# Differential attention beside an fp8 feed-forward block on one core: square root table loaded by a dummy root, copies of the first stage in another order, last exponentials, scaling and projection by smaller parts

## The chip, the core and the metric

The kernel runs on one core of a Trainium2 chip. The metric is the time of one execution on the device, in microseconds (us). The core has five engines that run side by side, each through its own instructions in order: PE (TensorE, matmuls and transposes), ACT (ScalarE, activation functions and copies), DVE (VectorE, elementwise work and 32x32 transposes), POOL (GpSimd) and SP (here only a queue that issues DMAs). They wait for one another through semaphores: an instruction adds to one when it ends, and a wait holds its engine until the count is reached.

## The reference, cut to what matters

```python
xn   = layernorm(x)                                  # x: 1024 rows x 256
qkv  = xn @ Wqkv                                     # q1,k1,q2,k2 (128 wide each), v (256); 16 heads of 8
A1   = causal_softmax(q1 k1^T / sqrt(8)) v
A2   = causal_softmax(q2 k2^T / sqrt(8)) v
diff = A1 - lam * A2
diff = (1 - LAMBDA_INIT) * diff / sqrt(mean(diff^2, -1) + 1e-5)
attn = diff @ Wproj
ffn  = fp8dot(gelu(fp8dot(xn, Wg0)) * fp8dot(xn, Wg1), Wlin)   # hidden 1024
out  = x + attn + ffn
```

## The kernel before

All engines run programs written out by hand; no scheduler decides an order. There are four stages.

**1. Normalising, transposing, projecting.** x comes in eight blocks of 128 rows, in four DMAs of two blocks (the first pair as two DMAs). For pair i, DVE takes the statistics (`stats_of` L578, `spread_of` L583). ACT takes the square root (`root`, L417), DVE the reciprocal (`even_block`, L589), then DVE normalises the even block (L592) and ACT the odd one (`odd_block`, L424). PE transposes the pair into bank i of PSUM (`transposes`, L882), and ACT copies it from there into `xn_t` (`turned`, L430, semaphore `xt_out`). PE then multiplies with the weights of q1 and k1 (`queries_keys`, L902): units 0 and 1 are done with pairs 0 and 1, units 2 and 3 with pairs 2 and 3. Before its first transpose PE runs 11 matmuls on an identity (`WARM_UP`, L887), and behind it 3 more (`KEEP_UP`, L925). Each unit's sum is split in two: ACT copies its upper bits from PSUM to `parts` (`upper`, L436, `hi_ready`), DVE subtracts these and keeps the rest (`rest`, L616, `low_ready`). DVE also makes xn_t's fp8 copy in two halves (`x_to_fp8`, L621). ACT needs another function table for the gelu of stage 2, and has it loaded by a dummy activation (L455) between `upper(1)` and `upper(2)`.

**2. Feed-forward, upper half.** 16 steps n: four fp8 matmuls on PE (L958) into a pair of banks, gelu on ACT (L472), a product on DVE (L634). Step 0 waits for two `low_ready`, step 1 for four `xt_out`, step 2 for four `low_ready`, since they write the banks that stage 1 still reads. Bounds for the softmax are worked out beside it.

**3. Attention.** 96 units: PE makes three banks of scores (L1038), ACT takes one exponential over 128x1536 (L493), POOL masks the diagonal blocks, and PE multiplies with the values (L1050) some units later. DVE turns and divides the sums (`take` L709, `divide` L715 and L716), subtracts the branches, and POOL and PE do the rest of the projections and the feed-forward's lower half beside it.

**4. Ending.** The last exponential releases the last product (group 7, chunk 8; its four matmuls are 512 wide). DVE then does `take(7, 1)`, the last difference, the mean square; ACT the last root (L510); DVE the reciprocal, `scale_by_root(3, last)` (L753) and `turn_back(1, 1)` (L757). PE's `ending` waits for `turn_back(1, 0)` (third `out_t_ready`), does ten matmuls of the output projection (L1081) and one of the residual (L1086), waits for `turn_back(1, 1)` (fourth) and does the last four (blocks 4 to 7). DVE and ACT add or copy, and DMAs carry the result out.

Of the kernel before, what the change touches and what calls it, by code (L numbers as in the profile page):

```python
# [7 lines left out]
ACT = mybir.ActivationFunctionType  # L8
# [7 lines left out]
P = 128  # L16
T = 1024
C = 256
# [7 lines left out]
BR = 2  # L26
# [41 lines left out]

V_BANK = (6, 7, 6, 7)

WARM_UP, KEEP_UP = 11, 3

Y_BANK = (7, 7, 0, 0, 2, 2, 3, 4)

# [53 lines left out]
def diff_attention_ffn_kernel(nc, x, w_qkv, w_proj, lq1, lk1, lq2, lk2, w_gating, w_linear, out):  # L128
# [3 lines left out]
    with ExitStack() as ctx:  # L132
# [276 lines left out]
        @block.scalar  # L409
        def _(act):  # L410
            act.dma_start(x_sb[:, 1, :], x_rows[:, 1, :]).then_inc(x_in[0], 16)
            for b in (2, 6):
                act.dma_start(x_sb[:, b:b + 2, :], x_rows[:, b:b + 2, :]).then_inc(x_in[b // 2], 16)

            def root(i):
                act.wait_ge(var_ready, 2 * i + 2)
                act.activation(rstd[:, 1, 2 * i:2 * i + 2], mean_var[:, 2 * i:2 * i + 2, 1], ACT.Sqrt, bias=eps[:, 0:1]  # L417
                               ).then_inc(root_ready, 1)

            def odd_block(i):  # L420

                b = 2 * i + 1
                act.wait_ge(moved_ready, i + 1)
                act.activation(xn[:, b, :], x_sb[:, b, :], ACT.Identity, bias=rstd[:, 3, b:b + 1],  # L424
                               scale=rstd[:, 2, b:b + 1]).then_inc(odd_ready, 1)

            def turned(i):

                act.wait_ge(xt_ready, i + 1)
                act.activation(xn_t[:, :, i * C:(i + 1) * C], ps[:, i, :].rearrange("p (k n) -> p k n", k=KC), ACT.Copy  # L430
                               ).then_inc(xt_out, 1)

            def upper(u):
                i, h = QK_UNITS[u]
                act.wait_ge(qk_ready, u + 1)
                act.activation(parts[:, i, 0, h * HALF:(h + 1) * HALF], ps[:, QK_BANK[u], :], ACT.Copy  # L436
                               ).then_inc(hi_ready, 1)

            act.wait_ge(eps_set, 1)
            root(0)  # L440
            odd_block(0)
            turned(0)
            root(1)
            odd_block(1)
            root(2)
            turned(1)
            odd_block(2)
            root(3)
            turned(2)
            odd_block(3)  # L450
            upper(0)
            turned(3)
            upper(1)

            act.activation(lam_w[:, 6:7], rstd[:, 1, 0:1], ACT.Gelu_apprx_tanh)  # L455
            upper(2)
            upper(3)

            def move_longest(u):

                act.activation(norm_most[0:32, 0, u:u + 1], norm_most[32 * u:32 * u + 32, 0, 0:1], ACT.Copy
                               ).then_inc(norms_moved, 1)

            def move_shift(u):

                act.activation(shift[32 * u:32 * u + 32, 0, 1, :], shift[0:32, 0, 1, :], ACT.Copy).then_inc(shift_ready, 1)

            for n in range(len(FFN)):
                act.wait_ge(up_ready, n + 1)
                if n >= RING:  # L470
                    act.wait_ge(hidden_ready, n - RING + 1)
                act.activation(gated[:, n % RING, :], ps[:, 2 * PAIR[n], :], ACT.Gelu_apprx_tanh  # L472
                               ).then_inc(gelu_ready, 1)

                if n == 4:
                    act.wait_ge(norms_taken, 1)
                if 4 <= n < 7:
                    move_longest(n - 3)
                if n == 12:
                    act.wait_ge(shift_low, 1)  # L480
                if 12 <= n < 15:
                    move_shift(n - 11)
            act.wait_ge(dots_ready, 2)
            act.activation(lam_w[:, 2:4], lam_w[:, 0:2], ACT.Exp).then_inc(lam_exp, 1)

            for n in range(UNITS):
                br, hg, at = n // BRANCH, n // STEPS % HG, n * PER_UNIT % (KEPT * J)
                if n % BRANCH == 0:
                    act.wait_ge(shift_ready, 3 * (br + 1))
                if n * PER_UNIT < KEPT * J and at + PER_UNIT > KEPT * J - 2:  # L490
                    act.wait_ge(hidden_ready, len(FFN))
                act.wait_ge(scores_ready, n + 1)
                act.activation(probs[:, at:at + PER_UNIT, :].rearrange("p s u -> p (s u)"),  # L493
                               ps[:, 3 * (n % 2):3 * (n % 2) + 3, :].rearrange("p b n -> p (b n)"),
                               ACT.Exp, bias=shift[:, br, 1, hg * BR + br:hg * BR + br + 1], scale=SCALE
                               ).then_inc(exp_done, 1)

            def whole(b):

                act.wait_ge(y_ready, 4 if b == 6 else 1)  # L500
                at = C if b == 1 else 0
                act.activation(y[:, b, :], ps[:, Y_BANK[b], at:at + C], ACT.Copy).then_inc(y_copied, 1)


            act.activation(newton[:, 1, 112:113], newton[:, 0, 0:1], ACT.Sqrt)
            for b in (0, 1):
                whole(b)
            act.wait_ge(eps_set, 2)
            act.wait_ge(ms_ready, 1)
            act.activation(newton[:, 3, 112:128], newton[:, 2, 112:128], ACT.Sqrt, bias=root_eps[:, 0:1], scale=ROOT_SCALE  # L510
                           ).then_inc(rms_ready, 1)
            whole(6)
            act.wait_ge(y_copied, 3)
            act.dma_start(out_rows[:, 6, :], y[:, 6, :]).then_inc(y_out, 16)
# [58 lines left out]
        def _(dve):  # L573
# [35 lines left out]
            spread_of(3)  # L609
            even_block(3)  # L610

            def rest(u, bank):
                i, h = QK_UNITS[u]
                cols = slice(h * HALF, (h + 1) * HALF)
                dve.wait_ge(hi_ready, u + 1)
                dve.tensor_tensor(parts[:, i, 1, cols], ps[:, bank, :], parts_f32[:, i, 0, cols], ALU.subtract  # L616
                                  ).then_inc(low_ready, 1)

            def x_to_fp8(h):
                dve.wait_ge(xt_out, 2 * (h + 1))  # L620
                dve.tensor_copy(x8[:, :, h * HALF:(h + 1) * HALF], xn_t[:, :, h * HALF:(h + 1) * HALF],  # L621
                                saturate=False).then_inc(x8_ready, 1)

            x_to_fp8(0)
            rest(0, QK_BANK[0])
            x_to_fp8(1)
            rest(1, QK_BANK[1])
            rest(2, QK_BANK[2])
            rest(3, QK_BANK[3])

# [119 lines left out]
            def scale_by_root(i, b):  # L750
                n = b.stop - b.start
                s = slice(32 * i + b.start, 32 * i + b.stop)
                own.step(dve.tensor_tensor(fin[:, b, i, :], attn1[:, i, b, :],  # L753
                                           root[:, s].unsqueeze(2).broadcast_to([P, n, DV]), ALU.mult))

            def turn_back(p, h):
                dve.transpose(out_t[:, p, h * HALF:(h + 1) * HALF],  # L757
                              fin[:, 16 * h:16 * h + 16, 2 * p:2 * p + 2, :].rearrange("p b g d -> p b (g d)")
                              ).then_inc(out_t_ready, 1)

            def values_in(b):
# [79 lines left out]
            inverse_root(slice(0, 64))  # L841
            scale_by_root(0, all_of)
            scale_by_root(1, all_of)
            turn_back(0, 0)
            turn_back(0, 1)
            own.step(difference(2, 0))
            mean_of(2, 0)
            take(6, 1)
# [5 lines left out]
            inverse_root(slice(64, 112))  # L854
            scale_by_root(3, first)
            scale_by_root(2, all_of)
            turn_back(1, 0)
            take(7, 1)
            difference(3, 1).then_inc(ms_ready, 1)
            dve.wait_ge(rms_ready, 1)  # L860
            own.step(dve.reciprocal(root[:, 112:128], u[:, 112:128]))
            scale_by_root(3, last)
            turn_back(1, 1)
            dve.wait_ge(res_ready, TB // 2)
            for b in (2, 4):
                dve.wait_ge(y_ready, b // 2 + 1)
# [6 lines left out]
        def _(pe):  # L873
# [181 lines left out]
            def values(g, c):  # L1055
                if c in DIAGONALS:
                    pe.wait_ge(masked, diagonals_until(g, c))
                else:
                    pe.wait_ge(exp_done, g * STEPS + last_unit(c) + 1)
                (kb, wide, q0), *more = CHUNKS[c]  # L1060

                if g == 0 and c == 0:
                    pe.wait_ge(v_out, 6)
                if c == 0 and g > 0:
                    pe.wait_ge(o_taken, 2 * g)
                ins = product(g, c, 0, kb, wide, q0, c == 0)
                if c in (MIXED, LAST):
                    ins.then_inc(o_ready, 1)
                elif more:
                    product(g, c, wide * P, *more[0], False)  # L1070
# [53 lines left out]
            def ending():  # L1124
# [15 lines left out]
                residual(6)  # L1140
                pe.wait_ge(out_t_ready, 4)
                project(4, 1)
                for b in (5, 6, 7):
                    project(b, 1).then_inc(y_ready, 1)

            def second_branch(general):
# [45 lines left out]
```

## Time and profile before

| | us |
|---|---|
| median of 3 runs | 185.56 (185.2 to 185.72) |
| the profiled execution, its own time | 185.81 |
| its span, first to last instruction | 184.1 |
| ACT busy | 163.2 (89%) |
| PE busy | 177.2 (96%) |
| DVE busy | 90.9 (49%) |
| POOL busy | 63.5 (35%) |

The span is the time between the first and the last instruction of the profiled execution; the 1.7 us beside it lie outside of all instructions. A busy share is an average over the four stages, and PE's records overlap, so it says little of which engine sets the end. For that the chain of waits is read, which follows the last instruction back to what released it. In a timeline a row gives start, length, engine, line, and in brackets the idle time before it with what ended it. An fp32 matmul leaves two records, a matmul in fp8 or bf16 one.

### The profile page before, as it was taken

What the parts mean: (1) busy time and instruction counts of PE and PEld (TensorE: products, weight loads), DVE (VectorE), ACT (ScalarE), POOL (GpSimd) and SP (SyncE); (2) the same over time, 40 slices, a digit from 0 to 9 for tenths busy, and PEclk for the clock granted to TensorE, in tenths of its full rate; (3) what the DMA queues carried; (4) which work ended last, traced back from release to release, by engine and by line L of the source; (5) the groups of instructions that cost most, each with busy time, mean ns of one, the idle gap of its engine ahead of it and who ended that gap; (6) DMA issues with size and microseconds to landing.
All of it is one profiled execution on the core that took longest, in us unless ns stands there. A gap on an engine that the chain in (4) does not pass through costs nothing.

```text
span 184.1 us, 4290 instructions
## 1 busy us (share of the span) xinstructions
PE 177.2 (96%) x1810; PEld 77.3 (42%) x1810; DVE 90.9 (49%) x216; ACT 163.2 (89%) x145; POOL 63.5 (35%) x81
## 2 busy tenths in 40 slices
PE   6899999999999999999999999999999999989992
PEld 6787344443332423243334424334524434433381
DVE  2485879432313150440365022616551789979872
ACT  0678587999999999999999999999999999999810
POOL 8319950051207321450523053307403560323000
PEclk9999999999999999999999999999999999999999
DMA  5987658874000000000087876000000000000015
GB/s 170 382 307 226 164 144 193 213 166 108 0 0 5 0 0 4 0 0 4 15 204 171 207 164 166 0 0 4 4 0 0 4 0 4 0 0 4 0 57 178
DMA packets 8935, 15.02 MB, mean 82 GB/s; under 512 B 2000, under 2 KB 5584, under 8 KB 8912
## 3 DMA queue, kind: packets, MB, share of 16 engines
q1 hardware_dynamic: 8080, 13.92, 27.8%
q10 hardware_dynamic: 832, 0.79, 1.3%
q8 instruction: 16, 0.26, 0.6%
q14 instruction: 7, 0.06, 0.1%
HBM read 5.26 MB, written 1.05 MB: 34 GB/s over the span
## 4 chain that ended last, share of the span: by engine, by line
ACT 77%; PE 18%; DVE 2%; DMA 1%; issue 1%; ACTq 0%
ACT probs L493 74%; PE ps L958 7%; PE ps L1081 4%; PE ps L902 3%; PE ps L892 2%; DMA x_sb<-L_attn_x 1%; PE ps L882 1%; DVE parts L616 1%; ACT L455 1%; ACT L417 1%; PE ps L1050 1%; ACT parts L436 1%; PE ps L1038 0%; DVE stats L578 0%; PE ps L925 0%
## 5 line engine op out<-in xcount | busy, mean ns | idle before, releaser
L493 ACT ACTIVATE probs<-ps,shift 128x1536 f32<-128x1536 f32 x96 | 138.0, 1599 | 0.2 <-PE ps L1038 0.2
L1050 PE MATMUL ps<-probs,v_all 128*32 128x512 f32 (+3 forms) x768 | 78.3, 496 | 1.1 <-DVE o_t L709 0.8
L393 POOL TENSOR_SCALAR_AFFINE_SELECT probs<-probs 128x1024 f32<-128x1024 f32 (+1 forms) x40 | 36.7, 918 | 94.8 <-ACT probs L493 94.8
L1038 PE MATMUL ps<-q_st,k_st 32*128 32x512 f32 (+3 forms) x384 | 48.4, 411 | 0.0
L1038 PEld LDWEIGHTS ps<-q_st,k_st 32*128 32x128 f32 x384 | 22.5, 182 | 61.5 <-ACT probs L493 43.4
L709 DVE STREAM_TRANSPOSE o_t<-ps 128x512 f32<-128x512 f32 x16 | 11.5, 717 | 45.3 <-PE ps L1050 45.2
L1050 PEld LDWEIGHTS ps<-probs,v_all 128*32 128x32 f32 x768 | 16.2, 108 | 18.8 <-issue 9.5
L958 PE MATMUL ps<-area 128*128 128x512 fp8e4 x64 | 14.4, 379 | 0.2 <-DVE parts L616 0.2
L472 ACT ACTIVATE probs<-ps 128x512 bf16<-128x512 f32 x16 | 9.6, 597 | 3.5 <-PE ps L958 2.9
L634 DVE TENSOR_TENSOR area<-ps,probs 128x512 fp8e4<-128x512 f32 x16 | 10.9, 685 | 1.9 <-ACT probs L472 1.8
L355 POOL TENSOR_TENSOR squares<-parts 128x512 bf16<-128x512 f32 x8 | 8.7, 1099 | 2.1 <-DVE parts L773 2.1
L958 PEld LDWEIGHTS ps<-area 128*128 128x128 fp8e4 x64 | 6.0, 97 | 8.1 <-issue 0.9
L892 PE MATMUL ps<-area 128*32 128x256 fp8e4 x256 | 9.2, 273 | 0.0
L892 PE MATMUL ps<-xn_t,w_q 128*32 128x256 f32 (+1 forms) x88 | 9.0, 482 | 0.0
L773 DVE CAST parts<-ps 128x512 fp32r<-128x512 f32 x4 | 2.8, 692 | 12.5 <-PE ps L892 12.5
L892 PE MATMUL ps<-w_q,xn_t 128*32 128x256 f32 x128 | 8.4, 384 | 0.0
L902 PE MATMUL ps<-xn_t,w_q 128*128 128x256 f32 x32 | 7.9, 390 | 0.1
L1081 PE MATMUL ps<-w_p,squares 128*128 128x256 f32 x32 | 7.7, 389 | 0.0
L892 PEld LDWEIGHTS ps<-area 128*32 128x32 fp8e4 x256 | 6.7, 97 | 2.3 <-issue 0.5
L778 DVE CAST ffn<-ps 128x512 bf16<-128x512 f32 x4 | 2.8, 691 | 9.2 <-PE ps L892 9.2
L362 POOL CAST area<-probs 128x512 fp8e4<-128x512 f32 x8 | 4.9, 658 | 6.1 <-DVE probs L592 6.1
L1081 PEld LDWEIGHTS ps<-w_p,squares 128*128 128x128 f32 x32 | 5.8, 190 | 2.0 <-DVE squares L757 1.2
(88 smaller groups left out, 128.0 us busy)
## 6 DMA issues: line engine op xcount, KB each, us to landing
q_st<-parts SPq DMA_DIRECT2D x32, 128.0 KB, 2.7
k_st<-parts SPq DMA_DIRECT2D x32, 128.0 KB, 2.8
probs<-L_ffn_w_gating SPq DMA_DIRECT2D x4, 512.0 KB, 7.3
probs<-L_ffn_w_linear SPq DMA_DIRECT2D x1, 1024.0 KB, 12.7
out<-probs SPq DMA_DIRECT2D x3, 256.0 KB, 2.3
x_sb<-L_attn_x ACTq DMA_DIRECT2D x2, 256.0 KB, 5.0
w_q<-L_attn_Wqkv SPq DMA_DIRECT2D x1, 512.0 KB, 9.1
w_q<-L_attn_Wqkv SPq DMA_DIRECT2D x1, 256.0 KB, 3.8
```

What stands on the lines that cost most here:

```text
L355: pool.tensor_tensor(squares[:, i, cols], parts_f32[:, i, 0, cols], parts_f32[:, i, 0, cols], ALU.mult).then_inc(squared, 1)
L393: pool.affine_select(out=blocks, in_=blocks, pattern=pattern, compare_op=ALU.is_ge, fill=0.0, base=0, channel_multiplier=-1).then_inc(mask ...
L472: act.activation(gated[:, n % RING, :], ps[:, 2 * PAIR[n], :], ACT.Gelu_apprx_tanh).then_inc(gelu_ready, 1)
L493: act.activation(probs[:, at:at + PER_UNIT, :].rearrange("p s u -> p (s u)"), ps[:, 3 * (n % 2):3 * (n % 2) + 3, :].rearrange("p b n -> p ...
L634: dve.tensor_tensor(hidden[:, c, h * HALF:(h + 1) * HALF], ps[:, 2 * PAIR[n] + 1, :], gated[:, n % RING, :], ALU.mult, saturate=False).the ...
L709: dve.transpose(o_t[:, h, :, :].rearrange("p b w -> p (b w)"), ps[:, 6, :]).then_inc(o_taken, 1)
L892: ins = pe.matmul(ps[q:q + 32, bank, at:at + right.shape[-1]], left[:, q:q + 32], right, start=start, stop=stop, skip_group_check=True)
L902: return pe.matmul(ps[:, bank, at:at + wide], w_q[:, k, i * P:(i + 1) * P], xn_t[:, k, h * HALF + at:h * HALF + at + wide], start=(k == 0 ...
L958: ins = pe.matmul(ps[:, 2 * PAIR[n] + g, :], w_gate8[:, g, k, c * P:(c + 1) * P], x8[:, k, h * HALF:(h + 1) * HALF], start=(k == 0), stop= ...
L1038: ins = pe.matmul(ps[:, bank, at:at + wide * P], k_st[rows, g % STACKS, kb * P:(kb + 1) * P], q_st[rows, g % STACKS, queries], start=True, ...
L1050: ins = pe.matmul(ps[32 * j:32 * j + 32, 6, q0 % HALF:q0 % HALF + wide * P], v_all[:, g % HG, kb, 32 * j:32 * j + 32], probs[:, slot + j, ...
L1081: return pe.matmul(ps[:, Y_BANK[b], at:at + C], out_t[:, p, b * P:(b + 1) * P], w_p[:, p, :], start=start, stop=(p == 1), skip_group_check ...
```

## The change

- ACT runs a dummy square root as soon as `eps` is set, before it waits for any statistics.
- `WARM_UP` is 10 instead of 11.
- `turned(3)` is done by DVE, between `rest(0)` and `rest(1)`; `rest(1)` now stands before `x_to_fp8(1)`.
- The dummy gelu stands between `upper(0)` and `upper(1)`.
- The last exponential (n = 95) is two activations of 128x3x256; the last product is two of half the width, each waiting for its own.
- `scale_by_root(3, last)` and `turn_back(1, 1)` are done in two halves of 8 blocks, and PE's last four projections wait in two pairs.

```diff
-WARM_UP, KEEP_UP = 11, 3
+WARM_UP, KEEP_UP = 10, 3
@@ ACT
             act.wait_ge(eps_set, 1)
+            act.activation(lam_w[:, 7:8], eps[:, 0:1], ACT.Sqrt)
             root(0)
...
             upper(0)
-            turned(3)
+
+            act.activation(lam_w[:, 6:7], rstd[:, 1, 0:1], ACT.Gelu_apprx_tanh)
             upper(1)
-
-            act.activation(lam_w[:, 6:7], rstd[:, 1, 0:1], ACT.Gelu_apprx_tanh)
             upper(2)
...
+                for e in range(1 if n < UNITS - 1 else 2):
+                    cols = slice(e * C, (e + 1) * C) if n == UNITS - 1 else slice(0, HALF)
+                    act.activation(probs[:, at:at + PER_UNIT, cols], ps[:, 3 * (n % 2):3 * (n % 2) + 3, cols],
+                                   ACT.Exp, bias=shift[:, br, 1, hg * BR + br:hg * BR + br + 1], scale=SCALE
+                                   ).then_inc(exp_done, 1)
@@ DVE
+            def turned(i):
+
+                dve.wait_ge(xt_ready, i + 1)
+                dve.tensor_copy(xn_t[:, :, i * C:(i + 1) * C], ps[:, i, :].rearrange("p (k n) -> p k n", k=KC)
+                                ).then_inc(xt_out, 1)
...
             rest(0, QK_BANK[0])
+            turned(3)
+            rest(1, QK_BANK[1])
             x_to_fp8(1)
-            rest(1, QK_BANK[1])
             rest(2, QK_BANK[2])
...
-            scale_by_root(3, last)
-            turn_back(1, 1)
+            for b in (16, 24):
+                scale_by_root(3, slice(b, b + 8))
+                turn_back(1, b, 8)
@@ PE
+                if (g, c) == (GROUPS - 1, NC - 1):
+                    product(g, c, 0, kb, 2, q0, False)
+                    pe.wait_ge(exp_done, UNITS + 1)
+                    product(g, c, 2 * P, kb, 2, q0 + 2 * P, False).then_inc(o_ready, 1)
+                    return
...
                 project(4, 1)
-                for b in (5, 6, 7):
+                project(5, 1).then_inc(y_ready, 1)
+                pe.wait_ge(out_t_ready, 5)
+                for b in (6, 7):
                     project(b, 1).then_inc(y_ready, 1)
```

ACT's order at the start and at the end of stage 1. First the program before, from its first DMA; `rstd` is the root's output, `parts<-ps` is `upper`, `xn_t<-ps` is `turned`:

```order
L411 DMA x_sb<-L_attn_x 128x256
L413 DMA x_sb<-L_attn_x 128x2x256 x2
L417 ACT_TABLE_LOAD [waits var_ready]
L417 ACTIVATE rstd<-mean_var,eps 128x2 [waits eps_set]
...
L436 ACTIVATE parts<-ps 128x512 [waits qk_ready]
L430 ACTIVATE xn_t<-ps 128x2x256 [waits xt_ready]
L436 ACTIVATE parts<-ps 128x512 [waits qk_ready]
L455 ACT_TABLE_LOAD
L455 ACTIVATE lam_w<-rstd 128x1
L436 ACTIVATE parts<-ps 128x512 [waits qk_ready] x2
```

And the same places now:

```order
L411 DMA x_sb<-L_attn_x 128x256
L413 DMA x_sb<-L_attn_x 128x2x256 x2
L441 ACT_TABLE_LOAD
L441 ACTIVATE lam_w<-eps 128x1 [waits eps_set]
L417 ACTIVATE rstd<-mean_var,eps 128x2 [waits var_ready]
...
L436 ACTIVATE parts<-ps 128x512 [waits qk_ready]
L455 ACT_TABLE_LOAD
L455 ACTIVATE lam_w<-rstd 128x1
L436 ACTIVATE parts<-ps 128x512 [waits qk_ready] x3
```

The first table load no longer stands behind the wait for the variances, and one copy (`turned(3)`) has left the stretch between the last odd block and the gelus, where the load has moved one place up.

DVE at the end of stage 1, before (from `x_to_fp8(0)` to the first product of the feed-forward):

```order
L621 CAST area<-xn_t 128x2x512 [waits xt_out]
L616 TENSOR_TENSOR parts<-ps,parts 128x512 [waits hi_ready]
L621 CAST area<-xn_t 128x2x512 [waits xt_out]
L616 TENSOR_TENSOR parts<-ps,parts 128x512 [waits hi_ready] x3
L634 TENSOR_TENSOR area<-ps,probs 128x512 [waits gelu_ready] x3
```

and now:

```order
L630 CAST area<-xn_t 128x2x512 [waits xt_out]
L625 TENSOR_TENSOR parts<-ps,parts 128x512 [waits hi_ready]
L618 COPY xn_t<-ps 128x2x256 [waits xt_ready]
L625 TENSOR_TENSOR parts<-ps,parts 128x512 [waits hi_ready]
L630 CAST area<-xn_t 128x2x512 [waits xt_out]
L625 TENSOR_TENSOR parts<-ps,parts 128x512 [waits hi_ready] x2
L644 TENSOR_TENSOR area<-ps,probs 128x512 [waits gelu_ready] x3
```

DVE has one instruction more there, and its second `rest` no longer stands behind the second cast.

PE's last instructions, before (values, projection, residual, projection):

```order
L1050 MATMUL ps<-probs,v_all 32x512 [waits exp_done]
L1050 MATMUL ps<-probs,v_all 32x512 x3
L1081 MATMUL ps<-w_p,squares 128x256 [waits out_t_ready]
L1081 MATMUL ps<-w_p,squares 128x256 x9
L1086 MATMUL ps<-x_sb,ident 128x256 [waits res_ready]
L1081 MATMUL ps<-w_p,squares 128x256 [waits out_t_ready]
L1081 MATMUL ps<-w_p,squares 128x256 x3
```

and now:

```order
L1062 MATMUL ps<-probs,v_all 32x256 [waits exp_done]
L1062 MATMUL ps<-probs,v_all 32x256 x3
L1062 MATMUL ps<-probs,v_all 32x256 [waits exp_done]
L1062 MATMUL ps<-probs,v_all 32x256 x3
L1098 MATMUL ps<-w_p,squares 128x256 [waits out_t_ready]
L1098 MATMUL ps<-w_p,squares 128x256 x9
L1103 MATMUL ps<-x_sb,ident 128x256 [waits res_ready]
L1098 MATMUL ps<-w_p,squares 128x256 [waits out_t_ready]
L1098 MATMUL ps<-w_p,squares 128x256
L1098 MATMUL ps<-w_p,squares 128x256 [waits out_t_ready]
L1098 MATMUL ps<-w_p,squares 128x256
```

The last product has become two of half the width, and the last two projections have a wait of their own; the eleven matmuls between keep their places.

## Rows read from the trace of the kernel before

**Rows 1.** The page: span, and the chain that ended last, by engine.

```profile
span 184.1 us, 4290 instructions
ACT 77%; PE 18%; DVE 2%; DMA 1%; issue 1%; ACTq 0%
```

**Rows 2.** The chain of waits in order of time: start us, us, what.

```profile
4.69 1.28 ACT L417
...
18.02 1.30 DVE parts L616 x2
...
103.55 68.95 ACT probs L493 x48
...
172.54 1.06 PE ps L1050 x8
173.61 4.51 PE ps L1081 x20
178.12 0.43 PE ps L1086 x2
```

**Rows 3.** Timeline of ACT, 0 to 26 us: start us, us, engine, line, what.

```profile
1.24 1.00 ACTq L413 DMA_DIRECT2D x_sb<-L_attn_x  x2
4.69 1.28 ACT L417 ACT_TABLE_LOAD   x1 [4.69 <-DVE mean_var L583]
5.98 0.30 ACT L417 ACTIVATE rstd<-mean_var,eps 128x2 f32<-128x2 f32 x1
...
13.63 0.58 ACT L436 ACTIVATE parts<-ps 128x512 fp32r<-128x512 f32 x1
14.90 0.60 ACT L430 ACTIVATE xn_t<-ps 128x512 f32<-128x512 f32 x1 [0.69 <-PE ps L882]
...
16.00 1.28 ACT L455 ACT_TABLE_LOAD   x1
...
17.41 1.07 ACT L436 ACTIVATE parts<-ps 128x512 fp32r<-128x512 f32 x2
```

**Rows 4.** Timeline of PE, 0 to 30 us.

```profile
1.61 5.06 PE L887 MATMUL ps<-ident 128*128 128x128 f32 x22 [1.61 <-POOL ident L336]
7.05 0.97 PE L882 MATMUL ps<-ident,probs 128*128 128x128 f32 x4 [0.38 <-DVE probs L592]
...
8.80 1.10 PE L902 MATMUL ps<-xn_t,w_q 128*128 128x256 f32 x4
...
17.38 1.89 PE L958 MATMUL ps<-area 128*128 128x512 fp8e4 x8
19.45 1.89 PE L958 MATMUL ps<-area 128*128 128x512 fp8e4 x8 [0.18 <-DVE parts L616]
```

**Rows 5.** PE's lines L887 and L925: ns min/median/max of a record, first and last start.

```profile
L887 PE MATMUL ps<-ident x22: 421/421/582, 1.6 to 6.3; 128*128 128x128 f32 x22
...
L925 PE MATMUL ps<-ident x6: 275/275/275, 7.9 to 8.4; 128*128 128x128 f32 x6
```

**Rows 6.** Tile x_sb: all DMAs into it, issue to landing.

```profile
DMA to landing us min/median/max: 2.3/4.2/5.7
```

**Rows 7.** Timeline of DVE, 0 to 33 us.

```profile
6.59 0.41 DVE L592 TENSOR_SCALAR probs<-x_sb,mean_var,rstd 128x256 f32<-128x256 f32 x1
6.91 0.74 DVE L578 BATCH_NORM_STATS2 stats<-x_sb 128x6 f32<-128x256 f32 x2
...
14.25 0.69 DVE L616 TENSOR_TENSOR parts<-ps,parts 128x512 fp32r<-128x512 f32 x1 [0.77 <-ACT parts L436]
```

**Rows 8.** Timeline of PE's weight loads, 15.0 to 15.7 us.

```profile
15.55 0.30 PEld L902 LDWEIGHTS ps<-xn_t,w_q 128*128 128x128 f32 x2 [0.22 <-ACT xn_t L430]
```

**Rows 9.** Timeline of DVE, 170 to 182 us.

```profile
172.71 0.71 DVE L757 STREAM_TRANSPOSE squares<-xn_t 128x512 f32<-128x512 f32 x1
173.67 0.72 DVE L709 STREAM_TRANSPOSE o_t<-ps 128x512 f32<-128x512 f32 x1 [0.25 <-PE ps L1050]
...
177.29 0.42 DVE L753 TENSOR_TENSOR xn_t<-attn,newton 128x256 f32<-128x256 f32 x1
177.75 0.71 DVE L757 STREAM_TRANSPOSE squares<-xn_t 128x512 f32<-128x512 f32 x1
```

**Rows 10.** The page's groups: out<-in xcount, busy us, mean ns of one.

```profile
L493 ACT ACTIVATE probs<-ps,shift 128x1536 f32<-128x1536 f32 x96 | 138.0, 1599 | 0.2 <-PE ps L1038 0.2
```

More of the change, by code:

```diff
@@ L492, in _ @@
                 act.wait_ge(scores_ready, n + 1)
[L493 to L496, printed above, removed]
+                for e in range(1 if n < UNITS - 1 else 2):
[3 more added lines that the diff above has]
+                                   ).then_inc(exp_done, 1)
             def whole(b):
@@ L754, in scale_by_root, with turn_back @@
                                            root[:, s].unsqueeze(2).broadcast_to([P, n, DV]), ALU.mult))
-            def turn_back(p, h):
-                dve.transpose(out_t[:, p, h * HALF:(h + 1) * HALF],
-                              fin[:, 16 * h:16 * h + 16, 2 * p:2 * p + 2, :].rearrange("p b g d -> p b (g d)")
+            def turn_back(p, first, n):
+                dve.transpose(out_t[:, p, 32 * first:32 * (first + n)],
+                              fin[:, first:first + n, 2 * p:2 * p + 2, :].rearrange("p b g d -> p b (g d)")
                               ).then_inc(out_t_ready, 1)
@@ L843, in _ @@
             scale_by_root(1, all_of)
-            turn_back(0, 0)
-            turn_back(0, 1)
+            turn_back(0, 0, 16)
+            turn_back(0, 16, 16)
             own.step(difference(2, 0))
@@ L856, in _ @@
             scale_by_root(2, all_of)
-            turn_back(1, 0)
+            turn_back(1, 0, 16)
             take(7, 1)
```

## The prediction

> **What bounds the kernel now.** I read the chain of waits first. ACT has 77% of it [rows 1], nearly all exponentials: the last 48 take 68.95 us [rows 2], 1.436 us each without a gap, and the change leaves 95 of the 96 as they are. So the exponentials are a block of fixed length; the change can only move its start (stages 1 and 2) and shorten what follows it (the ending). I went on with the timelines of PE, ACT and DVE in these two stretches.
>
> In stage 1 the chain has a table load of 1.28 us on ACT at 4.69, ahead of the first root [rows 2, 3]. Everything behind it waits: the first root, DVE's first block, ready at 6.59 + 0.41 = 7.00 [rows 7], the transposes at 7.05, the projections at 8.80, and from there PE works nearly without a pause until feed-forward step 1 [rows 4]. The next break is before step 2 at 19.45, where DVE's last `rest` is awaited [rows 2, 4]. Behind it PE sets the pace up to the exponentials. In the ending PE is the chain again from 172.54 on: product 1.06, ten projections 4.51, residual 0.43, the last four [rows 2].
>
> **The first table load.** The dummy root needs only `eps` and stands behind ACT's DMA issues, which end at 1.24 + 1.00 = 2.24 [rows 3]. The load then ends near 3.5, the dummy (at most 0.30, as a root [rows 3]) near 3.8, ahead of 4.69 when the variances are there. So the real root starts 1.29 earlier, and DVE's first block is ready at 5.71 in place of 7.00. PE isn't free then. The warm-up records take 421 ns and start every 0.21 (22 from 1.6 to 6.3 [rows 5]). With 20, the next record can start at 6.3 - 0.2 = about 6.05. So the transposes move from 7.05 to 6.05 and no further. Had 11 been kept, it would be about 6.45; the tenth is what the smaller `WARM_UP` pays for, 0.4 at most.
>
> They also run slower there. The records say which rate PE had: 421 ns for a 128x128 record until the transposes, 275 ns for the same shape from 7.9 [rows 5]; that is the lower (1.2 GHz) and the higher (2.4 GHz) of the clock's levels, and the change of level falls into the first transposes. In the changed kernel all four records of these run at the low rate: last start 6.05 + 3 x 0.21 = 6.68, end 7.10. In the kernel before the last ended at 7.05 + 0.97 = 8.02 [rows 4]. ACT's copy (0.60 as at 14.90 [rows 3]) ends at 7.73 and the projection could start at 7.88, by the same 0.15 that it took before. But the six keep-up records start from 6.89 on at 0.21, four or five of them at the low rate if the level changes at about the same moment, so PE is free at about 7.95. That is 0.85 before 8.80. With the level changing later all six are slow: free at 8.17, a gain of 0.63, and up to 0.2 more is lost in the first projection; with an earlier change 7.88, a gain of 0.92. Ends: 0.4 and 1.1. I take 0.85.
>
> The Trainium skill ("TensorE: Matmul & The Clock Gate", Part 1: The HAM clock gate) says that the warm-up is a budget of time and not a number of matmuls, which speaks against this edit: work brought forward is work at the low rate. The trace agrees as far as it can, with 421 and 275 ns. Without it (all at the high rate) the sum would have 0.92 here.
>
> Does the rest of stage 1 follow? Each pair's chain on ACT and DVE starts from the one before it and shifts with it. What could hold it is a landing: pair 1 of x is issued at 1.24 [rows 3] and DMAs into x_sb take 2.3 to 5.7, median 4.2 [rows 6], so it is there at 5.4 by the median. Its statistics began at 6.91 [rows 7] and would now begin at 5.63. A tie, in which I see no loss; the case with 5.7 is a rival. Later pairs are asked for later than they land even then.
>
> **The reordered copies.** `turned(3)` began on ACT at 14.90 and took 0.60 [rows 3]; PE's weight load waited for it, 0.22, until 15.55 [rows 8]. So it lies on the path. On DVE it stands behind `rest(0)`, which ended at 14.25 + 0.69 = 14.94 [rows 7]. No copy of this form is in the trace; the nearest row is that `rest`, 128x512 out of PSUM in 0.69. Bounds 0.6 and 0.8. It ends at 15.62 by the old clock, against 15.50: PE loses 0.12.
>
> In exchange ACT has its table load behind `upper(0)` (ends 14.21): load until about 15.45, dummy 0.20, `upper(1)` until about 16.2, and `rest(1)` until 16.85. Step 0 begins 0.12 later than 17.38, at 17.50, so that is in time. `upper(2)` and `upper(3)` no longer stand behind the load, which before held them until 17.41 and 17.95 [rows 3]. Unit 3's sum ends at about 17.65, `upper(3)` at 18.25, the last `rest` at 18.95. Eight records of steps 0 and 1 start 0.216 apart (1.73): step 2 could begin at 17.50 + 1.73 = 19.23, and is no longer held by DVE. Before it began at 19.45 [rows 4]. Net gain of this part 0.22, the lost 0.12 included. Ends: a loss of 0.1 (copy 0.8, step 2 still held) and a gain of 0.35.
>
> From step 2 on the order of work is the same on all engines, so steps, bounds, first scores and first exponential shift as a whole: 0.85 + 0.22 = 1.07.
>
> **The ending.** One exponential takes 1.60 as a record and 1.436 in the row of them [rows 2, 10], so each start costs some 0.15, and two halves end 0.1 to 0.2 later than one. The first half of the last product runs beside the second exponential, and the whole ends at about 173.2 in place of 172.54 + 1.06 = 173.60 [rows 2]. Who was waiting? PE's projections need `turn_back(1, 0)`, which ends at 172.71 + 0.71 = 173.42 [rows 9] whatever the product does; they began at 173.61 and will begin at 173.53 or so. DVE's `take(7, 1)` began at 173.67 after an idle 0.25 [rows 9] and can start at 173.45, 0.22 earlier. So of 0.4 that the split frees, PE gets 0.07 and DVE 0.22.
>
> DVE's scaling and turning took 177.29 to 178.46 [rows 9], and PE's residual ended at 178.12 + 0.43 = 178.55 [rows 2]: a tie. PE starts a record before the last one has ended, so without a wait it would have gone on at about 178.4. The halves (nearest rows: 0.42 and 0.71 for twice the size; bounds 0.21 and 0.42, 0.36 and 0.71; I take 0.29 and 0.45) give the first pair at 177.07 + 0.74 = 177.8 and the second by 178.6, at worst 179.3, while PE asks for them at 178.35 and 179.2. PE thus never waits: its last four start at about 178.35 to 178.4 in place of 178.52. Gain 0.13. The splitting's extra DVE instructions lie beside PE's eleven matmuls; without that cover they'd cost up to 0.5. The ends are a gain of 0.45 (all of the split arrives) and a loss of 0.2.
>
> **Sum.** 0.85 + 0.22 + 0.13 = 1.20 from 185.81, the profiled execution's own time: 184.61. It stood 0.25 above the median of the runs; from 185.56 the sum gives 184.36, and 184.3 to 184.4 is the forecast.
>
> **Rivals.**
> A. *The second pair of x lands late.* With 5.7 from issue it is there at 6.94, its statistics begin when they did before, and PE's second transposes with them: of the 0.85 only 0.1 stays. 185.56 - 0.1 - 0.22 - 0.13 = 185.1. For it: the maximum of 5.7; against: the two DMAs on this queue were issued in order, and the later one has the longer way.
> B. *The ending's split arrives in full*, since DVE's chain and not PE's decides there in the undisturbed run (they are within 0.1 of each other). 184.36 - 0.32 = 184.04.
> C. *The load between `upper(0)` and `upper(1)` comes too late*: if the copy behind a table load had to wait beyond it, by as much as a load (1.28), `upper(1)` would end at 17.5, `rest(1)` at 18.15, step 0 begin near 18.3 and step 2 at 20.03, a loss of 0.58 where I forecast a gain of 0.22: 184.36 + 0.8 = 185.2. Against it: the root began 0.01 after its load's end, 4.69 + 1.28 = 5.97 [rows 3]. The Trainium skill ("ScalarE: Activation LUTs", What ACT_TABLE_LOAD costs) puts a drain of 1.38 us behind each 1.28 us load; with that figure in place of the 1.28 the time would be 185.3; this trace shows the load but no such drain.
> D. *Slower: PE stays at the low rate in the projections.* 10 warm-ups in place of 11, then work brought forward. From 7.95 on every microsecond of work at the high rate costs another. The gain of 1.2 is used up if the level changes 2.4 us behind that point, at 10.4, and at 11.5 the kernel is 0.3% slower: 186.1. Against: PE had its pause (0.38 at 7.05 [rows 4]) and changed level all the same, and now has none.
> E. *Nothing arrives*: stage 2 turns out to be held by something that doesn't move. 185.5.
>
> **How the numbers follow.** The forecast 0.66 (184.34, its own range 183.9 to 184.8), A 0.09, B 0.10, C 0.04, D 0.04, E 0.07. 0.3% is 0.56 us, about what a measurement of this kernel can tell from no change: faster means below 185.0. The forecast, B and a part of A are faster, the rest of A, C and E within it, D and a rest of E slower: faster 0.81, same 0.14, slower 0.05. The range reaches from B's lower side to A: 183.7 to 185.1.
>
> **What would show it.** In the changed trace: the load at about 2.3; the first transposes near 6.05, not 5.8; the first projection near 7.95; DVE's copy ending 0.1 later against PE than ACT's did; no idle time before step 2; the exponentials about 1.07 earlier; DVE's last `take` 0.2 earlier against the last exponential; PE without idle time from its first projection of the ending to the last. I am wrong if the first projection moves by less than 0.4 or the ending by more than 0.3.

## The result, and the profile after

The changed kernel takes 184.63 us (median of 6 runs, 184.12 to 185.0), against 185.5 (6 runs, 185.2 to 185.72): ratio 0.9953, 95% interval 0.9933 to 0.9973, so 0.5 to 1.2 us faster. A second set of 6 runs on another occasion had 184.36 and 0.9931 (0.9918 to 0.9944). The runs of the changed kernel spread over 0.9 us, those of the kernel before over 0.5. A ratio leaves out executions more than 1.5% above the fastest of their kernel; of all that follow that is one, of 188.92.

The profiled execution took 184.12, its span 182.3, which is the fastest of the six; against its counterpart (185.81) it gained 1.69. The stretches it is made of are read below. First ACT's timeline in stage 1, then PE's, to be held against [rows 3, 4]:

```profile
2.27 1.28 ACT L441 ACT_TABLE_LOAD   x1 [2.27 <-issue]
...
4.75 0.30 ACT L417 ACTIVATE rstd<-mean_var,eps 128x2 f32<-128x2 f32 x1 [0.97 <-DVE mean_var L586]
```

```profile
5.82 0.74 PE L894 MATMUL ps<-ident,probs 128*128 128x128 f32 x4 [0.32 <-DVE probs L595]
...
7.34 1.10 PE L914 MATMUL ps<-xn_t,w_q 128*128 128x256 f32 x4
...
16.02 1.89 PE L970 MATMUL ps<-area 128*128 128x512 fp8e4 x8
18.06 1.89 PE L970 MATMUL ps<-area 128*128 128x512 fp8e4 x8 [0.15 <-DVE parts L625]
```

The load is out of the way. The first projection starts at 7.34 in place of 8.80, 1.46 earlier; the prediction had 7.95. Feed-forward step 0 starts 8.68 behind it (before 8.58), step 2 2.04 behind that (before 2.07), with PE still waiting for DVE. So of the 1.46 there are 1.39 left at step 2 and 1.40 at the second exponential (34.63 in place of 36.04). The reason stands in DVE's timeline:

```profile
13.44 0.69 DVE L618 COPY xn_t<-ps 128x512 f32<-128x512 f32 x1
14.79 0.69 DVE L625 TENSOR_TENSOR parts<-ps,parts 128x512 fp32r<-128x512 f32 x1 [0.66 <-ACT parts L436]
15.39 1.32 DVE L630 CAST area<-xn_t 128x1024 fp8e4<-128x1024 f32 x1
16.64 1.27 DVE L625 TENSOR_TENSOR parts<-ps,parts 128x512 fp32r<-128x512 f32 x2
```

The copy takes 0.69, as forecast, but the second cast takes 1.32; at its old place it took 0.69. The last `rest` therefore ends at 17.91, and step 2 waits for it.

The ending, as the chain of waits has it, and then DVE's last `take` in its timeline, to be held against [rows 2, 9]:

```profile
171.30 0.72 DVE squares L768
172.02 0.04 issue
172.07 4.58 PE ps L1098 x20
176.65 0.43 PE ps L1103 x2
177.08 1.74 PE ps L1098 x8
178.82 0.02 issue
178.85 0.42 DVE probs L882
```

```profile
171.98 0.72 DVE L719 STREAM_TRANSPOSE o_t<-ps 128x512 f32<-128x512 f32 x1
```

Ahead of these rows this chain no longer runs over the last exponential but over DVE's difference, iteration and scaling of group 7: it is DVE that now says when the ten projections begin. PE has no pause in its 15 matmuls. The last addition (L882) is 1.70 earlier than its counterpart at 180.55. The last exponential's start is 1.42 earlier (169.50 in place of 170.92), so the ending gained 0.28. The forecast had 0.13.

### The profile page after: what moved, and what is told of

It is laid out like the page before. It is cut to its first block, busy times and chain, and to the rows that moved or that the text cites. A ratio compares the mean times of both kernels' runs of the same rounds, so it can differ in the third digit from the quotient of the medians.

```text
span 182.3 us, 4305 instructions
## 1 busy us (share of the span) xinstructions
PE 175.5 (96%) x1816; PEld 76.3 (42%) x1816; DVE 92.4 (51%) x219; ACT 163.2 (90%) x146; POOL 63.5 (35%) x81
## 3 DMA queue, kind: packets, MB, share of 16 engines
HBM read 5.26 MB, written 1.05 MB: 35 GB/s over the span
## 4 chain that ended last, share of the span: by engine, by line
PE 82%; DVE 11%; ACT 2%; DMA 2%; issue 1%; DVEq 0%
PE ps L1062 35%; PE ps L1050 20%; PE ps L904 12%; PE ps L970 7%; PE ps L1098 4%; DVE o_t L719 2%; PE ps L914 2%; DMA x_sb<-L_attn_x 2%; DVE parts L625 1%; PE ps L894 1%; PE ps L1103 1%; DVE parts L737 1%; ACT L455 1%; DVE area L630 1%; DVE xn_t L763 1%
## 5 line engine op out<-in xcount | busy, mean ns | idle before, releaser
L497 ACT ACTIVATE probs<-ps,shift 128x1536 f32<-128x1536 f32 (+1 forms) x97 | 138.1, 1582 | 0.2 <-PE ps L1050 0.2
```

The source lines that it names most:

```text
L497: act.activation(probs[:, at:at + PER_UNIT, cols], ps[:, 3 * (n % 2):3 * (n % 2) + 3, cols], ACT.Exp, bias=shift[:, br, 1, hg * BR + br:hg ...
```

## The experiments

Every kernel was timed in turn with the kernel before; the ratio is to that, and 0.1% is 0.19 us.

**The three parts alone, and all of it again.** The first is

```diff
-WARM_UP, KEEP_UP = 11, 3
+WARM_UP, KEEP_UP = 10, 3
...
+            act.activation(lam_w[:, 7:8], eps[:, 0:1], ACT.Sqrt)
             root(0)
```

> The kernel before with the dummy root and 10 warm-ups alone. My theory (the start pays 0.85, more where PE's clock has risen before the transposes, less where it rises after): 0.6 to 1.4 us faster, and a profile whose first projection starts at 7.3 if the record of the warm-ups shrinks to 275 ns before 5.7, near 7.95 if it doesn't. The exponentials begin earlier by just what the first projection does. Rival (the start pays its whole 1.29 in every execution, and the middle or the ending loses some of it): 1.3 us faster whatever the records' lengths.

Measured: 184.84, ratio 0.9948 (0.9929 to 0.9966), 0.6 to 1.3 us faster. The profiled execution shows what neither theory said. Its first projection is at 7.09, 1.71 earlier than before, but step 0 is 9.38 behind it and not 8.58, so only 0.91 of that is left. DVE's timeline:

```profile
6.30 0.75 DVE L579 BATCH_NORM_STATS2 stats<-x_sb 128x6 f32<-128x256 f32 x2 [0.71 <-DMA x_sb<-L_attn_x]
...
7.62 0.43 DVE L579 BATCH_NORM_STATS2 stats<-x_sb 128x6 f32<-128x256 f32 x1 [0.28 <-DMA x_sb<-L_attn_x]
```

And PE's:

```profile
8.69 0.75 PE L883 MATMUL ps<-ident,probs 128*128 128x128 f32 x4 [0.50 <-DVE probs L593]
```

Pairs 1 and 2 of x landed later than in the changed kernel's profile, DVE waited for both, and PE stood idle for 0.50 before its second transposes. That is rival A of the prediction, in part of the executions.

The second part alone:

```diff
             upper(0)
-            turned(3)
+
+            act.activation(lam_w[:, 6:7], rstd[:, 1, 0:1], ACT.Gelu_apprx_tanh)
             upper(1)
-
-            act.activation(lam_w[:, 6:7], rstd[:, 1, 0:1], ACT.Gelu_apprx_tanh)
...
             rest(0, QK_BANK[0])
+            turned(3)
+            rest(1, QK_BANK[1])
             x_to_fp8(1)
-            rest(1, QK_BANK[1])
```

> The kernel before with the copies' new order alone (turned(3) on DVE, dummy gelu one place up, the cast behind the second rest). As predicted: 0.2 faster. What the changed kernel's trace suggests instead: DVE's cast takes 1.3 us beside POOL's squares in place of 0.69, the last rest still holds step 2, and the part is worth 0 or a loss of 0.1. Second cast 1.3 us: the new reading; 0.69: the prediction's.

Measured: 185.74, 1.0004 (0.9994 to 1.0013). Nothing, or 0.1 to 0.2 either way; the predicted gain of 0.22 (0.9988) lies outside. So the prediction's term fails and the new reading holds: the second cast takes 1.33. DVE's cast, and POOL's squares beside it:

```profile
16.82 1.33 DVE L626 CAST area<-xn_t 128x1024 fp8e4<-128x1024 f32 x1
```

```profile
15.56 4.48 POOL L355 TENSOR_TENSOR squares<-parts 128x512 bf16<-128x512 f32 x4
```

The third part alone is the diff above from the last exponentials to the last projections.

> The kernel before with the ending's edits alone (two last exponentials, two last products, halves of scaling and turning, two waits of the projections). As predicted 0.13 faster; by the changed trace 0.3 faster, since PE starts its last four 0.19 earlier against the exponentials and SP's last issue follows 0.35 earlier. Rival (all of the split arrives): 0.45.

Measured: 185.37, 0.9985 (0.9975 to 0.9995): 0.28 faster (0.1 to 0.5). More than the term of 0.13, though that isn't excluded.

> The whole change again, in the same runs as its three parts. 0.9 us faster by the median so far. If the parts add up, this is the sum of the other three within 0.3. If PE's clock makes the spread (theory), a profile with the rise behind the transposes has a longer span than 182.3, by 0.6; if not, the span is near 182.3 again whatever the warm-ups' records say.

Measured: 184.36, 0.9931 (0.9918 to 0.9944), 1.28 faster. The parts' ratios add up to -0.0052 + 0.0004 - 0.0015 = -0.0063, 1.17: they add. The span was 182.3 again, but the clock rose at 5.47, ahead of the transposes (5.83), so this profile doesn't test whether a late rise makes a longer span.

**Does the landing of x hold the start?** Twice the suspected cost:

```diff
-            for b in (2, 6):
+            for b in (6, 2):
                 act.dma_start(x_sb[:, b:b + 2, :], x_rows[:, b:b + 2, :]).then_inc(x_in[b // 2], 16)
```

> The changed kernel with ACT's two x DMAs in the other order: pair 3 first, then pair 1. Theory (what the table load left, the landing of pair 1 now holds): pair 1 lands some 1 us later, near 6.7, its statistics begin when it lands, PE stands idle before its second transposes, and the kernel loses 0.7 to 1.3 against the changed one, so it is at or near the kernel before. Rival (the landings have slack, and the spread of the runs is PE's clock): under 0.3 lost.

Measured: 1.003 (1.0004 to 1.0056), six runs from 185.33 to 187.21 and the one of 188.92, whose mean granted clock is also the lowest of all (0.989; 0.995 or more in the others). The profile, of the run of 187.02, DVE first and then PE:

```profile
8.67 0.75 DVE L581 BATCH_NORM_STATS2 stats<-x_sb 128x6 f32<-128x256 f32 x2 [2.82 <-DMA x_sb<-L_attn_x]
```

```profile
10.81 0.74 PE L894 MATMUL ps<-ident,probs 128*128 128x128 f32 x4 [1.83 <-DVE probs L595]
```

The theory is right in kind. The loss is larger than I said, 1.4 to 1.8 against the changed kernel's two ratios. In the profile pair 1 landed at 8.6 and not 6.7. Then the suspected cost taken away, pair 1 in two DMAs right behind pair 0:

```diff
-            sp.dma_start(x_sb[:, 0, :], x_rows[:, 0, :]).then_inc(x_in[0], 16)
+            for b in (0, 2):
+                sp.dma_start(x_sb[:, b, :], x_rows[:, b, :]).then_inc(x_in[b // 2], 16)
...
-            for b in (2, 6):
-                act.dma_start(x_sb[:, b:b + 2, :], x_rows[:, b:b + 2, :]).then_inc(x_in[b // 2], 16)
+            for b in (1, 3):
+                act.dma_start(x_sb[:, b, :], x_rows[:, b, :]).then_inc(x_in[b // 2], 16)
+            act.dma_start(x_sb[:, 6:8, :], x_rows[:, 6:8, :]).then_inc(x_in[3], 16)
```

> The changed kernel with pair 1 of x in two DMAs of a block each, on both queues right behind the first pair's. Theory: pair 1 lands by 5.0 to 5.3, its statistics never wait for it, and the kernel is as fast as the changed one's best runs in every run: 1.3 to 1.5 faster than before, with a smaller spread. Rival (clock): no change in median or spread against the changed kernel, 1.1 faster than before.

Measured: 185.13, 0.9975 (0.9964 to 0.9987). Slower than the changed kernel: both expectations missed. Pair 1 was there in time, but pair 2, pushed back, was not. DVE's timeline:

```profile
5.64 0.75 DVE L582 BATCH_NORM_STATS2 stats<-x_sb 128x6 f32<-128x256 f32 x2
...
8.31 0.43 DVE L582 BATCH_NORM_STATS2 stats<-x_sb 128x6 f32<-128x256 f32 x1 [1.64 <-DMA x_sb<-L_attn_x]
8.65 0.15 DVE L593 RECIPROCAL rstd<-rstd 128x2 f32<-128x2 f32 x1
```

DVE's program has the statistics of block 4 ahead of `even_block(1)`. So an engine that waits for pair 2 keeps pair 1, ready long since, from being normalised. In the changed kernel's first profile the same wait is there with 0.20. In the kernel before there is none: the table load held DVE longer than that landing.

**The cast.** Back ahead of the second `rest`:

```diff
             turned(3)
-            rest(1, QK_BANK[1])
             x_to_fp8(1)
+            rest(1, QK_BANK[1])
```

> The changed kernel with DVE's second cast put back ahead of the second rest, behind turned(3). Theory (the cast takes 1.3 us only where POOL's squares run beside it): it starts about when they do, takes 0.69, the last rest ends 0.5 earlier, PE has no idle time before step 2 (0.3 earlier against the first projection), and the kernel is 0.3 faster than the changed one. Rival (the cast's length comes from its place behind the copy or the rest): 1.3 us again, the second rest is late and step 0 too, 0.2 slower than the changed one.

Measured: 184.87, 0.9954 (0.9941 to 0.9967), no better than the changed kernel. DVE's timeline, then POOL's:

```profile
14.43 1.56 DVE L630 CAST area<-xn_t 128x1024 fp8e4<-128x1024 f32 x1
15.91 1.90 DVE L625 TENSOR_TENSOR parts<-ps,parts 128x512 fp32r<-128x512 f32 x3
```

```profile
14.40 2.48 POOL L355 TENSOR_TENSOR squares<-parts 128x512 bf16<-128x512 f32 x2
```

The cast started 0.03 behind the squares and took 1.56; in the kernel before it started at 15.53, 0.06 ahead of them, and took 0.69, and the same in the start's run. Step 2 came 1.72 behind step 0, but step 0 now waited 0.29 for the second `rest`. The wish to start it in time failed, and this run alone looks just like its rival: over 1.3 us, step 0 late, no faster than the changed kernel.

The fourteen profiles taken together tell the two apart. In nine of them the second cast begins while a product of POOL's runs, and in all nine it ends 0.55 behind that product's end, though it started anywhere from 0.03 to 0.27 behind the product's start. In the three where it begins first (before, start alone, ending alone) it takes 0.69, and POOL's first product takes 1.52 to 1.53 in place of 1.03. So here the one that starts second is the one that takes longer, by about what the first still has to run, and the place in DVE's order matters only through the moment of the start. POOL's first product in the kernel before, and the one beside the cast in the changed kernel (started 15.13, ended 16.16; the cast 15.39 to 16.71):

```profile
15.59 1.53 POOL L355 TENSOR_TENSOR squares<-parts 128x512 bf16<-128x512 f32 x1
```

```profile
15.13 1.03 POOL L355 TENSOR_TENSOR squares<-parts 128x512 bf16<-128x512 f32 x1
```

A test without DVE's cast gives it to ACT, which had idle time there (0.60 before `upper(2)`):

```diff
             upper(1)
+            act.wait_ge(xt_out, 4)
+            act.activation(x8[:, :, HALF:T], xn_t[:, :, HALF:T], ACT.Copy, saturate=False).then_inc(x8_ready, 1)
             upper(2)
...
             rest(1, QK_BANK[1])
-            x_to_fp8(1)
```

> The changed kernel with xn_t's second fp8 cast on ACT, between upper(1) and upper(2), instead of on DVE. Theory (DVE's cast beside POOL's squares is what still holds step 2): DVE does the last rest right behind ACT's last upper, PE starts step 2 1.72 behind step 0 in place of 2.04, and the kernel is 0.2 to 0.3 faster than the changed one. Rival (the last rest waits for ACT anyway, and ACT is later by a cast of 1.0): step 2 2.0 to 2.3 behind step 0, no gain or 0.2 slower.

Measured: 184.55, 0.993 (0.9914 to 0.9945), lowest 183.75. Steps 0 to 3 run without a pause, and step 2 is 1.73 behind step 0. ACT's timeline, then PE's:

```profile
15.20 1.05 ACT L458 ACTIVATE area<-xn_t 128x1024 fp8e4<-128x1024 f32 x1
16.15 1.21 ACT L436 ACTIVATE parts<-ps 128x512 fp32r<-128x512 f32 x2
```

```profile
7.88 1.10 PE L915 MATMUL ps<-xn_t,w_q 128*128 128x256 f32 x4
...
16.57 3.62 PE L971 MATMUL ps<-area 128*128 128x512 fp8e4 x16
```

In the profile 0.31 is won between step 0 and step 2. Its span of 182.9 is still 0.6 above the changed kernel's: the clock rose late (6.99), which left the last exponential 0.28 later, and the span then ended 0.34 further behind it, with the last addition at the same distance. In the medians no difference from the changed kernel can be told (184.55 against 184.36 and 184.63 on other occasions).

**A combination**, of the two edits before this last one (pair 1 first, cast first), with PE's products of blocks 4 and 5 moved:

```diff
                 values_due(UNITS + 1, 0, GROUPS)
+                project(4, 0, start=True)
+                project(5, 0)
                 pe.wait_ge(out_t_ready, 3)
...
-                project(4, 0, start=True)
-                project(5, 0)
                 project(7, 0, start=True)
```

> The changed kernel with both edits above, and PE's products of blocks 4 and 5 with out_t's first half moved ahead of the wait for the third turn. The ending should gain 0.2 to 0.3 from that, as PE has them done in the time it waits, and DVE's turn comes 0.4 before PE asks. If all three theories hold: 0.3 + 0.3 + 0.2 faster than the changed kernel, 1.7 to 2.0 faster than before. If only the ending's does, 1.3.

Measured: 185.51, 0.9997 (0.9984 to 1.001): the two edits that fail alone fail together. Measured from the start of the last exponentials (170.56, in the changed kernel 169.50), the last four projections are 0.22 earlier and the last addition 0.23. But SP's last DMA issue is 0.39 later (timeline of SP):

```profile
178.69 2.27 SPq L327 DMA_DIRECT2D out<-probs  x2
181.00 0.47 SPq L329 DMA_DIRECT2D out<-probs  x1
```

In the changed kernel the first two issues began at 177.62 and ended 1.89 later, and the last began at 179.55. I took the closer issues for the reason, and the forecast for the best version rests on that. Other profiles don't bear it out. The cast-on-ACT kernel has the changed kernel's ending, and its issues stretch just as much:

```profile
177.91 2.25 SPq L326 DMA_DIRECT2D out<-probs  x2
180.20 0.48 SPq L328 DMA_DIRECT2D out<-probs  x1
```

Over the nine profiles with the changed kernel's ending SP's last issue begins 9.79 to 10.41 behind the start of the last exponentials, and the span ends 12.68 to 13.32 behind it. With the two products moved it is 10.45 and 13.17 here, 10.21 and 12.95 in the best version. So the additions come 0.23 earlier, and whether the end of the kernel does can't be told from this; why the issues vary stays open.

**DVE's order, and the warm-ups.** First the order:

```diff
             spread_of(1)
-            stats_of(4)
             even_block(1)
+            stats_of(4)
```

> The changed kernel with DVE's even_block(1) ahead of the statistics of block 4, which wait for pair 2's landing. Theory (pair 2's landing reaches the path only through DVE's order): pair 1's normalising starts as soon as its root is there, PE has no idle time before its second transposes unless pair 1 itself lands after 6.0, and the kernel is 0 to 0.3 faster than the changed one with fewer slow executions: 1.1 to 1.5 faster than before. Rival (pair 2's statistics then come late and move the idle time to the third transposes): same as the changed kernel or 0.2 slower.

Measured: 184.91, 0.9958 (0.9944 to 0.9972): the rival. PE's second transposes had no idle time though pair 1 landed at 6.2 (the clock rose late, at 6.76, and the first projection came at 7.78), but the stretch behind them is longer, since the next pair's statistics come later (PE's timeline; the second row took 1.98 in the changed kernel):

```profile
8.71 0.62 PE L894 MATMUL ps<-ident,probs 128*128 128x128 f32 x4
9.17 2.30 PE L914 MATMUL ps<-xn_t,w_q 128*128 128x256 f32 x8
```

Then `WARM_UP, KEEP_UP = 9, 1` on top of it:

> As the one above, with 9 warm-ups and 1 behind the first transposes in place of 10 and 3. Theory (where PE's clock is low, warm-ups and keep-ups hold the first projection, which started at 7.88 where the rate rose after 7 and at 7.34 where it rose before 6): the first projection at 7.1 to 7.5 whenever the rise comes, 0.1 to 0.4 faster than the one above. Rival (the pause lets the clock fall or rise later): projections in part at the low rate, 0.5 or more slower.

Measured: 184.73, 0.9944 (0.9931 to 0.9957), 0.26 better than without by the ratios, within their uncertainty. First projection at 7.54, where the rate rose at 6.94; PE now waited 0.41 for ACT's copy. So a little later than the 7.1 to 7.5 expected, and no harm from the shorter warm-up. The best version below has the same 9 and 1, its clock rose at 7.62, and its first projection came at 7.76: "whenever the rise comes" does not hold.

**The best version found**: the changed kernel with `even_block(1)` first, 9 and 1 warm-ups, the cast on ACT and the two products moved.

> The changed kernel with the three edits of the runs above (even_block first, 9 and 1 warm-ups, the cast on ACT) and PE's products of blocks 4 and 5 with the first half of out_t ahead of the wait for the third turn. If each theory holds, 0.1 + 0.2 + 0.25 + 0.2 faster than the changed kernel, 1.7 to 2.1 faster than before; if the ending's gain is eaten by the queue of the output DMAs, as the profile of the combined kernel suggests, 1.5 to 1.8.

Measured: 184.29, 0.9919 (0.9906 to 0.9932), 1.5 faster than before (1.3 to 1.75). That is the low end of the lower forecast (1.5 to 1.8). The changed kernel's 0.9931 (0.9918 to 0.9944) overlaps, so the step beyond the changed kernel isn't shown to be more than 0.

**The clock's part.** The trace has its own record of the time at which the granted clock rose. In the fourteen profiles it fell between 4.5 and 7.7, with no pattern that I can see. With the dummy root and 10 and 3 warm-ups:

| clock rises at | first transposes | first projection |
|---|---|---|
| 4.54 (changed) | 5.82 | 7.34 |
| 4.83 (start alone; its first statistics began 0.33 earlier) | 5.66 | 7.09 |
| 5.47 (changed, again) | 5.83 | 7.35 |
| 5.86 (cast first) | 5.96 | 7.34 |
| 6.65 (combined) | 6.04 | 7.72 |
| 6.76 (even block first) | 6.04 | 7.78 |
| 6.99 (cast on ACT) | 6.04 | 7.88 |
| 7.10 (pair 1 late) | 6.04 | 7.88 |
| 7.56 (pair 1 first) | 6.04 | 7.89 |

With 11 and 3 and no dummy root the first projection was at 8.73, 8.76 and 8.80 for rises at 5.13, 7.49 and 7.74. So the moment is worth 0.55 to the kernels with the dummy root and 0.07 to those without. Both profiles of the changed kernel itself had an early rise.

## Why the prediction held, point by point

184.3 to 184.4 was forecast; 184.63 and 184.36 were measured, both inside the range of 183.7 to 185.1 and below the 185.0 that "faster" meant.

*The start, 0.85.* Right in kind and about right in size: alone 0.97 (0.6 to 1.3). The transposes at 6.05 and the projection at 7.95 came out as 6.04 and 7.88 where the rise was as late as in the trace I had read. What I took as the ordinary case was one end of a range; I had given an earlier rise 0.07 more, and it is 0.55, since warm-ups, transposes and keep-ups all shrink. Two things can take the average back from the 1.46 of the profile, and the runs don't divide it between them: a late rise (cast on ACT: second transposes at 8.82 without a wait for x, in the changed kernel 8.28) and the landing of x (start alone: an early rise, and 8.69). The landing I called a tie "in which I see no loss" and made a rival of it with 0.09 for one pair. The 5.7 it was built on belonged to pair 3, the last in the queue; with the DMAs in their order pair 1 took 4.1 to 5.0. The runs show both pairs 1 and 2 on the path, the second through DVE's order, with 0 to 0.5 of idle PE in the profiles with that order. "Later pairs are asked for later than they land even then" was wrong for pair 2: its statistics began at 7.85, so 1.28 earlier is 6.57, and it landed at 6.67 already in the trace I had read (6.88 in the changed kernel's).

*The copies' order, 0.22.* This step failed. The sentence "the last `rest` at 18.95" counted the second cast with the 0.69 it had in the trace; moved behind the second `rest` it starts beside POOL's squares and takes 1.32. Step 2 stayed held by DVE. Measured alone: nothing (+0.07, -0.1 to +0.2). The rest of the step was right: the copy took 0.69 and cost PE 0.10, and the load in its new place held nothing. With the cast on ACT step 2 came 1.73 behind step 0, as I had said. The trace of the kernel before had rows that should have warned me. DVE's product over 128x256 on L727 takes 0.42 at its median, but in the timeline of the ending one of them, begun 0.03 behind a mask of POOL's, takes 1.34 and ends 0.27 behind the mask:

```profile
166.83 1.10 POOL L393 TENSOR_SCALAR_AFFINE_SELECT probs<-probs 128x1024 f32<-128x1024 f32 x1 [0.80 <-ACT probs L493]
166.86 1.34 DVE L727 TENSOR_TENSOR parts<-attn 128x256 f32<-128x256 f32 x1
```

*The ending, 0.13.* Undersized: 0.28 alone (0.1 to 0.5), 0.28 in the profiles. DVE's `take` came 0.27 earlier against the exponentials (forecast 0.22), ACT's end 0.16 later (0.1 to 0.2), PE's ten projections 0.05 earlier (0.07), the last four 0.18 (0.13). What I left out is that the first matmul after the wait is itself longer, 483 ns in place of 379, which is the 0.10 that lies between 0.18 at the last four and 0.28 at the last addition. The lines' own view over the last eight records (ns min/median/max), before and then after:

```profile
L1081 PE MATMUL ps<-w_p,squares x8: 379/379/483, 178.5 to 180.1; 128*128 128x256 f32 x8
```

```profile
L1098 PE MATMUL ps<-w_p,squares x8: 379/379/380, 176.9 to 178.4; 128*128 128x256 f32 x8
```

*The sum.* 1.20 from three terms; 0.9 and 1.3 on two occasions. The start's term was nearly right, the middle's too large by 0.3 and the ending's too small by 0.15, so the misses in part cancel, and that the total fits better than its terms is luck. Of the signs, the copy came as forecast, the last `take` nearly so (0.27 in place of 0.2), and PE had no pause in the ending; in the profile the transposes (5.82), the first projection (7.34), the exponentials (1.40 earlier) and the wait before step 2 did not. The rivals: A happens, per execution and in part; B is not told apart by the time of the ending's run (0.1 to 0.5), but the profiles have 0.28 and not its 0.45; C is refuted by `upper(1)` at 14.17, which is 0.12 behind the load's end at 14.05 with the dummy between them; D by every profile, the latest rise being 7.7; E by the result.

## What to carry to other kernels

When a stall at the start goes, ask what had time to land under it, and look in each engine's program for a wait of a later item that stands ahead of work on an earlier one: in-order engines pass that wait on. When an instruction is moved, its duration is not moved with it: look at what the other engines do at the new place, and which of them starts first. And one trace is one draw of the clock's rise and of the DMAs' landings; a term that hangs on either needs its two ends in the sum.

## What the runs showed that I had not expected

DVE's 128x1024 cast from fp32 to fp8 took 0.68 to 0.69 where it began ahead of POOL's fp32 products and 1.32 to 1.56 where it began behind the start of one, always ending about 0.55 behind the end of that product, while DVE's copy and subtraction out of PSUM of 128x512 kept their 0.69 in both cases. ACT did that cast in 1.05 in both profiles that have it there, each time beside POOL's products, and these kept their 1.04.

The order of the x DMAs moved the landings more than I expected: in three orders of issue pair 1 landed at 4.3, 5.6 and 8.6, and in the last case six runs of one kernel spread over 1.9 us, without the one of 188.92.

The time from the start of the last exponentials to the end of the span differs by 0.6 between nine profiles with the same ending, though the last addition comes 9.34 or 9.35 behind that start in all of them. That is as large as the clock's part. Only output DMAs are left behind the last addition, and no run here explains why they vary.
